# Gated cross-attention and a 16-expert layer on one core: the last attention tile, the hand-over between the stages, and the eviction of expert results

## What is computed

```python
x = x + tanh(g_xattn) * (softmax(q @ k.T * scale, masked) @ v @ Wo + bo)   # q of layernorm(x)
probs = sigmoid(layernorm(x) @ gate_w.T); top_vals, sel = top_k(probs, 2)
weights = top_vals / (top_vals.sum(-1) + 1e-6)
slot = where(ranks < capacity, sel * capacity + ranks, sentinel)           # ranks: running count by expert
h = gelu(padded[slot] @ w1[e]); out = (h @ w2[e])[slot] * weights          # capacity 320
x = x + tanh(g_ffn) * out.sum(over the 2 choices)
```

## Time and profile before

| | us |
|---|---|
| median of 3 runs | 339.35 |
| the profiled execution | 340.83 |
| its span | 339.1 |
| PE busy | 309.0 |
| DVE, ACT, POOL busy | 251.2, 208.7, 191.6 |
| mean granted clock | 0.97 of full |

### The profile page before, as it was taken

How to read it: one execution, slowest core, us unless ns; L and a number is a source line. 1 busy time by engine, 2 the same in 40 slices (tenths; PEclk the granted TensorE clock), 3 DMA queues, 4 the chain that set the end, 5 groups by cost and what they waited for, 6 DMA issues and landing times.

```text
span 339.1 us, 6268 instructions
## 1 busy us (share of the span) xinstructions
PE 309.0 (91%) x2080; PEld 267.1 (79%) x2080; DVE 251.2 (74%) x585; ACT 208.7 (62%) x570; POOL 191.6 (57%) x242
## 2 busy tenths in 40 slices
PE   8889999999999999999849999999999999999700
PEld 3646779888898888887724899999999999999700
DVE  2679887698889898989755398888888888887200
ACT  1646876887888888866451366666666666664300
POOL 8034576585777777788771005555555365665650
PEclk9999999999999999999978999999999999999965
DMA  5989999300111111111225837778887888853430
GB/s 151 284 243 295 202 190 179 115 16 18 47 47 50 60 53 63 62 49 64 78 94 138 260 103 201 203 205 207 211 214 216 213 210 212 219 73 40 49 46 8
DMA packets 40906, 45.68 MB, mean 135 GB/s; under 512 B 5461, under 2 KB 34666, under 8 KB 40874
## 3 DMA queue, kind: packets, MB, share of 16 engines
q1 hardware_dynamic: 33410, 35.78, 37.8%
q0 software_dynamic: 7424, 9.48, 15.3%
q10 hardware_dynamic: 40, 0.02, 0.0%
HBM read 28.02 MB, written 17.24 MB: 133 GB/s over the span
## 4 chain that ended last, share of the span: by engine, by line
PE 77%; POOL 9%; DVE 4%; issue 4%; ACT 3%; DVEq 0%; POOLq 0%; ACTq 0%
PE ps_scores L1372 17%; PE ps_out L1388 13%; PE ps_scores L1242 11%; PE ps_out L1271 10%; PE ps_misc L1195 5%; PE ps_pT L1356 3%; PE ps_pT L1219 3%; PE ps_misc L1398 2%; PE ps_misc L1397 2%; PE ps_scores L1236 2%; POOL out_dram L561 2%; POOL padded L467 1%; ACT probs L647 1%; PE ps_scores L1258 1%; POOL probs L499 1%
## 5 line engine op out<-in xcount | busy, mean ns | idle before, releaser
L561 POOL DMA_INDIRECT out_dram<-wqT,diag x48 | 73.5, 1531 | 77.7 <-DMA out_dram<-wqT,diag 39.0
L1372 PE MATMUL ps_scores<-value_t,score_t 128*128 128x320 f32 x384 | 59.1, 310 | 0.0
L1372 PEld LDWEIGHTS ps_scores<-value_t,score_t 128*128 128x128 f32 x384 | 56.5, 188 | 0.4 <-DVE value_t L1081 0.3
L1242 PE MATMUL ps_scores<-score_t,xn 128*128 128x512 f32 x192 | 54.0, 426 | 0.0
L1271 PE MATMUL ps_out<-value_t,pT 128*128 128x256 f32 x384 | 53.4, 288 | 0.6 <-DVE pT L970 0.6
L1271 PEld LDWEIGHTS ps_out<-value_t,pT 128*128 128x128 f32 x384 | 47.7, 189 | 1.7 <-issue 1.6
L1242 PEld LDWEIGHTS ps_scores<-score_t,xn 128*128 128x128 f32 x192 | 36.3, 189 | 7.0
L720 ACT ACTIVATE ps_scores<-ps_scores 128x640 f32<-128x640 f32 x30 | 20.6, 688 | 34.1 <-PE ps_scores L1372 33.9
L467 POOL DMA_INDIRECT padded<-z,slot_row x32 | 33.4, 1044 | 10.0 <-issue 7.1
L647 ACT ACTIVATE probs<-ps_scores,row_low 128x64 f32<-128x64 f32 x128 | 38.1, 328 | 0.4 <-DVE row_low L943 0.4
L1095 DVE CAST value_t<-ps_scores 128x640 fp32r<-128x640 f32 x30 | 24.7, 824 | 17.9 <-ACT ps_scores L720 17.8
(11 more groups left out here) (202 smaller groups left out, 634.8 us busy)
## 6 DMA issues: line engine op xcount, KB each, us to landing
raw<-in_L_ffn_w_dram SPq DMA_DIRECT2D x16, 512.0 KB
wo_sb<-in_L_ffn_w_dram SPq DMA_DIRECT2D x16, 512.0 KB
padded<-empty SPq DMA_DIRECT2D x2, 2064.0 KB, 28.8
diag<-padded SPq DMA_DIRECT2D x16, 258.0 KB
out_dram<-x SPq DMA_DIRECT2D x16, 128.0 KB
padded<-empty SPq DMA_DIRECT2D x1, 1032.0 KB, 30.7
diag<-padded SPq DMA_DIRECT2D x16, 64.5 KB
wq_sb<-in_L_xattn_Wq_dram SPq DMA_DIRECT2D x2, 512.0 KB, 8.6
```

The costliest lines, as they stand in the source:

```text
L561: pool.indirect_dma_start(out, bass.IndirectOffsetOnAxis(ap=xg[0:SLOTS[k], r, k, TOKEN:TOKEN + 1].bitcast(U32), axis=0), y[0:SLOTS[k], j, ...
L1242: op = pe.matmul(dst, xn[:, t % 2, a, c], mv, start=False, stop=last)
L1372: op = pe.matmul(ps_scores[:, f, 0:CAPACITY], w1_hl(p, a)[:, c, f * P:(f + 1) * P], x_hl(p, b)[:, c], start=c == 0 and (a, b) == PARTS[0], ...
```

## The change

- **Last tile's probabilities.** Those of tile 15 get a home of their own (`pT_last`, in the score weights, which are no longer read then), and its attention product goes to `ps_misc`. PE turns them inside the attention product of tile 14, and doesn't wait for `x1` of tile 14 before it starts tile 15.
- **Normalisations.** From tile 12 on the second norm is split: DVE makes minus the mean and the variance plus eps, POOL the power alone, ACT the shift (one more small operation). POOL normalises the probabilities of tile 15.
- **Order at the hand-over.** On DVE the last residuals and the low parts change places; on PE filler products go (5 to 2, 3 to none) and the router of tile 13 comes before the attention product of tile 14.
- **First rows on two queues.** ACT's queue issues the second gather of expert 0; PE waits only for the first two gathers of an expert, no longer for the 8-byte tails.
- **Result tiles.** For every expert each tile is evicted alone: ACT takes the first before it splits the second weights, and POOL adds it without waiting for the second. Tiles 0 and 2 share a bank, tile 1 has the other.

The diff, cut to its core:

```diff
@@ -224,7 +227,15 @@
         ps_zT = ps_misc[:, 0:DIM]
-        ps_attn = ps_out[:, 0:DIM]
+        def attn_of(t):
+            return ps_misc[:, 0:DIM] if t == LAST else ps_out[:, 0:DIM]
+        def pT_of(t, k):
+            return pT_last[:, k] if t == LAST else pT[:, k]
         ps_logits = ps_scores[:, 2, 0:32].rearrange("p (a e) -> p a e", a=2)
@@ -238,18 +249,11 @@
-        def near_end(e):
-            return e >= EXPERTS - 2
-        def y_bank(e, k):
-            n = SLOTS[k]
-            if k == 2:
-                return ps_misc[0:n, 0:DIM]
-            if near_end(e):
-                return ps_pT[0:n, k, 0:DIM] if e == EXPERTS - 2 else ps_scores[0:n, k, 0:DIM]
-            return ps_out[0:n, k * DIM:(k + 1) * DIM]
+        def y_tile(e, k):
+            if e == EXPERTS - 1:
+                return ps_scores[:, k, 0:DIM]
+            return ps_misc[:, 0:DIM] if k == 1 else ps_out[:, k // 2 * DIM:(k // 2 + 1) * DIM]
@@ -384,8 +389,9 @@
                                  ).then_inc(fetched[r], 16)
-                    sp.dma_start(xg[0:SLOTS[2], r, 2], padded[at + 2 * P:at + CAPACITY, :]).then_inc(fetched[r], 16)
-                    sp.dma_start(xg[SLOTS[2]:, r, 2, TOKEN:], padded[at + 2 * P:at + CAPACITY, TOKEN:]).then_inc(fetched[r], 16)
+                    if e > 0:
+                        sp.dma_start(xg[0:SLOTS[2], r, 2], padded[at + 2 * P:at + CAPACITY, :]).then_inc(fetched[r], 16)
+                    sp.dma_start(xg[SLOTS[2]:, r, 2, TOKEN:], padded[at + 2 * P:at + CAPACITY, TOKEN:]).then_inc(tailed[r], 16)
@@ -471,6 +477,9 @@
                 pool.wait_ge(stats2_ready, t + 1)
+                if t >= LATE_TILE:
+                    pool.tensor_tensor(l2[:, p, 1:2], l2[:, p, 0:1], power[:, 0:1], ALU.pow).then_inc(ln2_ready, 1)
+                    return
                 wait(pool, z2_ready, t - 1)
@@ -528,19 +539,23 @@
-            mark_tokens(PAIRS - 3)
             pool.wait_ge(slots_ready, PAIRS - 2)
-            dispatch(PAIRS - 3, 0, (0,))
+            dispatch(PAIRS - 3, 0)
             second_norm(LAST - 2)
-            dispatch(PAIRS - 3, 0, (1,))
+            p = LAST % 2
+            pool.wait_ge(norm_ready, TILES)
+            pool.tensor_tensor(probs[:, p], probs[:, p], norm[:, p, :, None].to_broadcast([P, HEADS, KEYS]),
+                               ALU.mult).then_inc(normed, 1)
             dispatch(PAIRS - 3, 1)
...
             mark_tokens(PAIRS - 1)
+            pool.wait_ge(slots_ready, PAIRS - 1)
+            dispatch(PAIRS - 2, 0, (0,))
             second_norm(LAST - 1)
-            pool.wait_ge(slots_ready, PAIRS - 1)
-            dispatch(PAIRS - 2, 0)
-            dispatch(PAIRS - 2, 1)
+            dispatch(PAIRS - 2, 0, (1,))
+            dispatch(PAIRS - 2, 1, (0,))
             second_norm(LAST)
+            dispatch(PAIRS - 2, 1, (1,))
             for k in range(2):
@@ -551,13 +566,14 @@
                 j, i, r = e % 2, e // 2, e % GATHERS
-                pool.wait_ge(fetched[r], 48 * (e // GATHERS + 1))
+                pool.wait_ge(fetched[r], 32 * (e // GATHERS + 1))
+                pool.wait_ge(tailed[r], 16 * (e // GATHERS + 1))
                 wait(pool, added[(j + 1) % 2], SLOT_TILES * 16 * (i + j))
...
                         pool.wait_ge(y_last, e + 1)
-                    elif near_end(e) or k == 0:
-                        pool.wait_ge(y_ready, 2 * e + k + 1 if near_end(e) else 2 * e + 2)
+                    else:
+                        pool.wait_ge(y_ready, 2 * e + k + 1)
                     pool.indirect_dma_start(out, bass.IndirectOffsetOnAxis(ap=xg[0:SLOTS[k], r, k, TOKEN:TOKEN + 1].bitcast(U32), axis=0),
@@ -604,23 +620,30 @@
-            def copy_probs(t):
-                for h in range(2):
+            def copy_probs(t, halves=(0, 1)):
+                for h in halves:
                     act.wait_ge(turned, 2 * t + h + 1)
-                    if h == 0:
+                    if t == LAST:
+                        act.wait_ge(scored, 2 * TILES)
+                    elif h == 0:
                         wait(act, attended, t)
-                    act.activation(pT[:, 0, 4 * h:4 * h + 4].rearrange("p c n -> p (c n)"), ps_pT[:, h],
+                    act.activation(pT_of(t, 0)[:, 4 * h:4 * h + 4].rearrange("p c n -> p (c n)"), ps_pT[:, h],
                                    ACT.Copy).then_inc(p_high, 1)
...
                 act.wait_ge(ln2_ready, t + 1)
+                bias = l2[:, p, 2:3]
+                if t >= LATE_TILE:
+                    bias = shift[:, p]
+                    act.activation(bias, l2[:, p, 2:3], ACT.Copy, scale=l2[:, p, 1:2]).then_inc(shifted, 1)
+                    act.wait_ge(shifted, t - LATE_TILE + 1)
                 if t >= RING:
...
                 act.activation(z2[:, t % RING, :, 0:DIM], x1[:, p, None, :].to_broadcast([P, 2, DIM]), ACT.Identity,
-                               bias=l2[:, p, 2:3], scale=l2[:, p, 1:2]).then_inc(z2_ready, 1)
+                               bias=bias, scale=l2[:, p, 1:2]).then_inc(z2_ready, 1)
@@ -685,15 +708,16 @@
-            copy_probs(LAST - 1)
+            copy_probs(LAST - 1, (0,))
             copy_x1(LAST - 2)
+            copy_probs(LAST - 1, (1,))
+            gate_exp(LAST - 2)
             second_rows(LAST - 3)
-            gate_exp(LAST - 2)
             second_rows(LAST - 2)
...
             copy_x1(LAST - 1)
+            gate_exp(LAST - 1)
             second_rows(LAST - 1)
-            gate_exp(LAST - 1)
             copy_x1(LAST)
@@ -710,6 +734,9 @@
                 if e == -1:
+                    for k in range(2):
+                        act.wait_ge(dispatched[k], 64 * PAIRS // 2)
+                    act.dma_start(xg[0:SLOTS[2], 0, 2], padded[2 * P:CAPACITY, :]).then_inc(fetched[0], 16)
                     for t in range(2):
@@ -729,25 +756,31 @@
+                def result(k):
+                    if exists(e, EXPERTS):
+                        act.wait_ge(y_made, SLOT_TILES * e + k + 1)
+                        act.activation(y[0:SLOTS[k], j, k], y_tile(e, k)[0:SLOTS[k]], ACT.Copy,
+                                       scale=xg[0:SLOTS[k], e % GATHERS, k, WEIGHT:WEIGHT + 1]).then_inc(y_ready, 1)
+                if exists(e, EXPERTS):
+                    wait(act, added[j], SLOT_TILES * 16 * i)
+                    act.wait_ge(fetched[e % GATHERS], 32 * (e // GATHERS + 1))
+                    act.wait_ge(tailed[e % GATHERS], 16 * (e // GATHERS + 1))
+                result(0)
                 for t in SPLIT_W2.get(e, (e + 2,)):
...
+                result(1)
                 if exists(e, EXPERTS):
-                    wait(act, added[j], SLOT_TILES * 16 * i)
-                    act.wait_ge(fetched[e % GATHERS], 48 * (e // GATHERS + 1))
-                    for k in range(SLOT_TILES):
-                        act.wait_ge(y_made, SLOT_TILES * e + (2 if k == 0 and not near_end(e) else k + 1))
-                        if k == SLOT_TILES - 1:
-                            wait(act, y_last, e)
-                            act.activation(y_low[:, :], ps_misc[SLOTS[k]:, 0:DIM], ACT.Copy,
-                                           scale=xg[SLOTS[k]:, e % GATHERS, k, WEIGHT:WEIGHT + 1]).then_inc(y_lowered, 1)
-                        else:
-                            act.activation(y[0:SLOTS[k], j, k], y_bank(e, k), ACT.Copy,
-                                           scale=xg[0:SLOTS[k], e % GATHERS, k, WEIGHT:WEIGHT + 1]).then_inc(y_ready, 1)
+                    act.wait_ge(y_made, SLOT_TILES * (e + 1))
+                    wait(act, y_last, e)
+                    act.activation(y_low[:, :], y_tile(e, 2)[SLOTS[2]:], ACT.Copy,
+                                   scale=xg[SLOTS[2]:, e % GATHERS, 2, WEIGHT:WEIGHT + 1]).then_inc(y_lowered, 1)
@@ -834,6 +867,15 @@
+            def second_stats(t):
+                p = t % 2
+                done.sync()
+                dve.wait_ge(z2_ready, t - 1)
+                done.done(dve.bn_aggr(mv2[:, p], stats2[:, :]))
+                dve.tensor_scalar(l2[:, p, 2:3], mv2[:, p, 0:1], -1.0, None, ALU.mult)
+                dve.tensor_scalar(l2[:, p, 0:1], mv2[:, p, 1:2], EPS, None, ALU.add).then_inc(stats2_ready, 1)
             def step(s, j, i):
@@ -1034,37 +1073,36 @@
             t, p = LAST, LAST % 2
+            place(PAIRS - 3, 0, 2, PAIRS - 2)
             dve.wait_ge(exped0, TILES)
             done.mark(dve.tensor_reduce(row_sum[:, p, 0:8], probs[:, p, 0:8], AX.X, ALU.add))
-            place(PAIRS - 3, 0, 2, PAIRS - 2)
             first_residual(LAST - 2)
...
             dve.wait_ge(normed, t - 1)
-            done.done(dve.tensor_scalar(norm[:, p], row_inv[:, :], nan, None, ALU.add))
+            dve.tensor_scalar(norm[:, p], row_inv[:, :], nan, None, ALU.add).then_inc(norm_ready, 1)
             low_probs(LAST - 1, 0)
             low_probs(LAST - 1, 1)
-            dve.tensor_tensor(probs[:, p], probs[:, p], norm[:, p, :, None].to_broadcast([P, HEADS, KEYS]), ALU.mult).then_inc(normed, 1)
...
```

(37 more changed lines are left out.)

41 lines of the change are left out of this document (24 added, 17 removed).

## The result

The changed kernel takes 343.11 us (median of 4 runs, 342.17 to 345.38), before beside it 339.43. The ratio is 1.0109, 95% interval 1.0078 to 1.0140: slower by 1.1%. The profiled execution took 342.17, span 340.3, and is the fastest of the four; the one of before lies 1.4 above its own median. So the two traces show 1.34 of a difference of some 3.7, and the rest has to come from the runs.

What follows compares the result with a forecast made beforehand. It took three pieces as the bound: expert choice for the last two tiles over POOL, 40 fillers at low clock, and POOL's chained adds. Routing 0.65, fillers and gather 0, result tiles 0.2: 339.35 - 0.85 = 338.5, range 336.5 to 340.1.

Steps and rivals of the forecast that it cites:

- The step that failed: Hand-over on PE: taking out the two groups of 3 fillers costs and gives nothing, since PE waits for residuals there.
- rival 4: Tile 14's product: fewer fillers let the clock fall during it, costing about 1.3 and giving 339.8; chance 0.06.
- The routing: Expert choice for the last two tiles: 0.14 plus 0.5 saved, 0.65 in sum; bounds 1.9 and a loss of 0.7.
- a second step that failed: From routing to the kernel's end: the 0.65 saved was subtracted in full from the final time.
- I expect that it falls: Clock at the 40 fillers: it drops as before, so they start and end 0.65 earlier at unchanged length.
- The thin stretch is no shorter: PE's thin activity in the last routing: argument against the clock staying up or recovering sooner, which would give 2.0.
- Rival 2: The 40 fillers: clock stays up or returns sooner, 9.15 instead of 11.15, giving 336.5; chance 0.10.
- First gather: Expert 0's first rows: second gather about 0.5 sooner and tails not awaited, both hidden behind the fillers, so 0.
- The forecast 0.2: Result tiles: the first add's lead of 1.9 fades within one or two experts, leaving 0.2; bounds 0 and 1.9.
- expert 13's adds: Near the end of the expert loop: these adds were to begin 0.3 to 0.8 after the second eviction.
- rival 3: Expert loop: early adds and weight loads hold each other up, expert 13's adds start 1.6 later, 340.3; chance 0.08.
- The rule on queues: DMA engines take queues in turn, so earlier adds would land sooner; the forecast held 0.2% against 94.3% speaks against it.

Runs made afterwards that it cites:

- old_fillers: The change with the two removed groups of filler products put back (5 for 2, 3 before tile 15's product): 340.87 us, ratio 1.0024 to before.
- handover_old: The change with result tiles handled as before and the two removed groups of fillers put back: 341.26 us, ratio 1.0040 to before.
- all_fillers: The change with the removed fillers put back, plus 8 behind tile 15's product and 11 behind its router: 338.52 us, ratio 0.9962 to before.
- before_late: The kernel before, with 12 filler products added behind the router of tile 15: 338.28 us, ratio 0.9951 to before.
- swap_alone: The kernel before, with SP's two weight loads issued in the other order and nothing else: 339.62 us, ratio 0.9997 to before.
- late_fillers: The change with 8 fillers added behind tile 15's product and 11 behind its router, removed ones not put back: 338.71 us, ratio 0.9973 to before.
- handover_alone: The change with result tiles handled as before, the removed fillers still out: 341.91 us, ratio 1.0062 to before.
- small_loads: The change with weight loads of experts 2 to 15 cut to 16 of 128 partitions (results differ): 339.46 us, ratio 0.9998 to before.
- pool_pairs: The change, but POOL alone waits for the second result tile before the first add of experts 0 to 13: 341.16 us, ratio 1.0052 to before.
- after_again: The change itself, unaltered, run once more on another chip: 342.67 us, ratio 1.0101 to before.
- wait_filler: The change with the removed fillers put back and 8 more behind tile 15's product, none behind its router: 341.76 us, ratio 1.0011 to before.

## Why the prediction was wrong

**The step that failed** is "the removed fillers of 3 and 3 cost nothing and give nothing here, as PE now waits for residuals in their places". I asked only whether PE waits there anyway. It does, 0.51 and 0.63, for low parts. But with the same result tiles, putting these fillers back is worth 2.6 us, of the 4.6 by which the forecast was off. The mechanism stood in rival 4, with a chance of 0.06 and 1.3 us. The traces show part of it. Tile 14's product does take 1.39 longer in a dip, and 0.67 of that is left when PE turns tile 15's `x1`: rival 4 priced the product and left out the wait that takes half of it. In the first trace there is no dip, and the low clock begins ahead of tile 15's router: 1.04 for 0.62, and the last count 0.54 later than in `old_fillers`. So 0.5 to 0.7 of the 2.6 stand in traces at the last count, and where the rest goes isn't shown. That this start of the low stretch is due to the fillers isn't shown either, as `handover_old` has them and the same start.

**The routing** was sized right as a path on PE: 0.65 forecast, 0.58 to 0.60 at the last count in all traces whose clock was up from tile 14's product to the router. That it would reach the end is a second step that failed. In the changed kernel 0.05 of it is left at the count, since the clock falls ahead of the router. The wait of 2.17 for tile 15's residual stands ahead of that, but it doesn't decide it alone: `old_fillers` has the same wait, and its clock falls behind the router. I wrote "I expect that it falls" of the clock for the fillers' sake alone, and not for the operations ahead of the last count, which are on the path. And where the clock is up throughout, the 0.6 is lost in the adds (`all_fillers` 0.9962, `before_late` 0.9951).

**The fillers.** "The thin stretch is no shorter" was right; that their length would stay was not. They take 9.97 to 11.57 in the traces whose low stretch reaches well into them, by where in it they begin. Rival 2 (the clock comes back sooner) thus seems half true in the profiled execution, 0.9 for its 2.0. But `swap_alone`, whose hand-over is that of before, has 10.05 from count to rows where the profile of before has 11.18: this much lies between executions of one hand-over, and the change needn't be its cause.

**First gather.** Hidden, as forecast: in the changed kernel the rows had landed at 183.9, before PE's turn at 185.8. With the clock up this cover is gone: in `late_fillers` they land at 183.07 and PE turns them at 183.12, so there a further cut in fillers would buy nothing.

**Result tiles.** The forecast 0.2 stands within what can be told where the fillers are in place (0.9986 alone; 0.9949 for 0.9951, and 0.9962 for 0.9962). On top of the hand-over without them, the tiles cost 1.3 to 1.6 us (1.0062 to 1.0101 and 1.0109), with intervals that just overlap; I had added up the parts as if each acted alone. The first add came at 200.31 (forecast 200.5), the middle experts' 2.0 to 3.3 after the second eviction (forecast 1 to 3), PE lost 1.26 at expert 15 (forecast 1.3). Not so expert 13's adds: 2.84 after the second eviction, forecast 0.3 to 0.8, since experts 9 and 11 were held by 1.8 and 0.8 and each later expert makes up only 8.23 - 7.78 = 0.45. What rival 3 priced came in this trace, 0.9 at expert 13 for its 1.6, but not by its mechanism: it asked for adds less than 1.1 after the second eviction, and expert 9's began 1.98 after it. Expert 9 takes 8.6 in `handover_alone` and `small_loads` too, with pairs and with small loads; what holds it isn't shown.

**The rule on queues.** The Trainium skill, DMA: Bandwidth & Descriptors, section on queues, rings and completion order, has each DMA engine take packets from its queues in turn. The rows of 204 to 206 speak against it again: no packet of the software queue, while the hardware queue has 97.8% of the engines. Whether packets of the software queue were ready by then, no trace shows. When the weight loads are cut, expert 0's adds take 7.6 from first issue to landing and not 10.2.

**What stays open.** With removed fillers, result tiles and hand-over together cost more (1.0109 and 1.0101) than the parts make (0.9986 and 1.0062: 1.0048). I have no trace that shows that rest of some 1.9 us. That POOL's pairs take half of the cost away points to the adds, though the trace of `pool_pairs` is no shorter there; that the median clock falls to 0.960 points to dips. But a dip left 0.67, and the mean clock isn't all: the profiled execution of `after_again` took 340.95, and four others 342.61 to 342.89, all at a mean clock of 0.959 to 0.961. Some 1.7 us of the median is thus in no trace. `old_fillers` lies 0.8 above before with a count 0.6 sooner; `wait_filler` points to PE's wait behind tile 15's product and doesn't settle it.

## What to carry to other kernels

A filler product ahead of a wait isn't free to remove because PE waits there anyway: ask what the clock will be for the next operation on the path, and price it at half speed, less the waits further on that take part of it up. Whoever shortens PE's work ahead of a fixed wait should try longer fillers there: with 8 and 11 more in the two waits of this hand-over the ratio went from 1.0024 to 0.9962; the 8 alone gave 0.4 us, less than can be told. And a lead given to a transfer lasts only until it meets the next burst of loads: follow it to the end of the chain before it is counted.

## What the runs showed of the hardware that I had not expected

Two executions of one kernel differ in where the clock is low: `after_again` has a dip at 159 to 162, where the first 15 products of tile 14 took 3.41 for 2.02, and the first profile of the change has none. Shortly ahead of that dip PE had been idle for 0.92 and for 0.51 alone, ahead of the first fall at 172 for 2.17. And an engine that is busy again isn't at full clock at once: in `handover_alone` PE ran 5.6 us of unbroken filler (176.08 to 181.7) at the low level, in the changed kernel 2.8. Eighteen recorded filler products in PE's waits of 2.2 and 2.4 us stand in the trace of `late_fillers`, whose clock stays up.
